# A state-space mixer on one Trainium2 core: the way from the input projection into the chunk loop, in another order

## The chip, the core and the metric

The kernel runs on one core of one Trainium2 chip. Such a core has five engines with an instruction queue each: TensorE (PE, matrix products; its weight loads are listed apart as PEld), VectorE (DVE), ScalarE (ACT), GpSimd (POOL) and SyncE (SP, which here only starts transfers). The queues run by themselves and meet at semaphores. The metric is the device time of one execution in microseconds (us), lower is better.

## The reference

The program is four blocks on one sequence of 1024 tokens with 256 features: a Mamba-like mixer with a feed-forward block, a factor mixing, a grouped-query attention and a mixture of experts. The change is in the mixer. Cut to what matters:

```python
h = _rmsnorm(hidden_states, ln1_w)
zxbcdt = h @ W_in                       # (1024 x 256) @ (256 x 770)
z, xv, Bv, Cv, dt = jnp.split(zxbcdt, splits, axis=-1)
xBC = jnp.concatenate([xv, Bv, Cv], axis=-1)          # 512 features
conv = sum((xp[:, k:k + l, :] * conv_w[k] for k in range(D_CONV))) + conv_b
xBC = jax.nn.silu(conv)
dt = jax.nn.softplus(dt + dt_bias)      # 2 columns, one for each head
a = -jnp.exp(A_log)
dA = dt * a
y = _ssd(xh * dt[..., None], dA, Bh, Ch, CHUNK)       # 8 chunks of 128 tokens
y = y + D[None, None, :, None] * xh
y = _rmsnorm(y * jax.nn.silu(z), norm_w)
h = res + y @ W_out
```

`_ssd` goes over the chunks; each needs cumulated sums of `dA`, exponentials of them, three products inside the chunk and a state that is handed to the next one.

## The kernel before

Each engine has its own hand-written program; the order of the work on an engine is the order of the code, and what it waits for is written as `wait_ge` on a semaphore.

**Projection.** The 1024 tokens are two groups (g = 0, 1) of 512. The 6 x 128 wide columns of `W_in` give twelve fills of a PSUM bank, in the order of `IN_FILLS`: q = 0 to 3 are the four blocks that are convolved (`CONV_BLOCKS`) for group 0, q = 4 to 7 the same for group 1, q = 8 to 11 the two blocks of z for both groups. Fill q goes to bank `2 + q % 4`, so that fill q waits for the evacuation of fill q - 4 (`s_evac`). On PE a fill is two matmuls of 128x512 (line 1409), and the trace has two records for each f32 matmul, so four records. Between fills 1 and 2 PE transposes the second group of normalised rows (line 1388). The two `dt` columns are 16 narrow matmuls of 128x2 (line 1403, 32 records), two for each of the eight tiles of 128 tokens, into bank 6; before, all of them stand ahead of fill 4, and the last one releases `s_dtp`.

**Evacuation, on ACT** (`projected`, lines 645 and 646): a fill that is convolved is copied to `xpad` and written once more as the last tap plus bias to `cv`; a fill of z goes through one Silu (line 642).

**Convolution, on DVE** (`convolve(g, pair)`, line 984): two blocks of one group, three taps each, so six instructions of 128x512. It waits for the evacuation of its two fills. ACT finishes it with a Silu for each block (`convolved(g, pair)`, line 656, `s_xbc`).

**Step sizes.** `dt` is a softplus, made as Exp on ACT (line 665), one added on DVE (line 998), Ln on ACT (line 670) and some ten small DVE instructions with 128x16 elements (lines 991 to 1012). The last gives `dA`. POOL makes the ramps of chunks 0 and 1 from it (line 490), PE two narrow products (lines 1416 and 1417), of which ACT takes the Exp (line 679), and DVE `dt` times the decay (line 1016), which POOL uses for `ddx` (line 505).

**Chunk loop.** For chunk c, `front(c)` on PE makes two transposes (line 1429), the segment sums (lines 1435 to 1437) and the product of B and C (line 1440). ACT copies the transposes to `tok` (line 693) and takes the Exp of the sums (line 695). DVE multiplies both with `dt` (`masked(c)`, line 1026). `back(c)` on PE makes the state and y (lines 1448 to 1456), and DVE and ACT finish them (lines 1045 to 1057, 685). `front(c + 1)` stands ahead of `back(c)`. The splits of the feed-forward weights (`ffn_w_hi` on ACT, `ffn_w_lo` on DVE) are done between chunks.

Table loads of ACT (ACT_TABLE_LOAD in the trace) are put in by the compiler where the next function isn't in the loaded set.

Of the kernel before, what the change touches and what calls it, by code (L numbers as in the profile page):

```python
# [29 lines left out]
ACT = mybir.ActivationFunctionType  # L30
# [4 lines left out]
TT = T // P  # L35
# [6 lines left out]
H_SSD = 2  # L42
N_IN = 770
CONV_BLOCKS = 4
# [29 lines left out]
def build(nc, x_in, small_in, const_in, w_in, w_out, f_w13, f_w2, factors, ffn_bias, wq, wk, wv, wo,  # L74
          gate, m_w1, m_w3, m_w2, m_w2t, out):
    slots_in = nc.dram_tensor("expert_in", [SLOT_TILES * P, SLOT_W], F32, kind="Internal").ap()
    with ExitStack() as ctx:
# [534 lines left out]
        def _(act):  # L612
# [51 lines left out]
            act.wait_ge(s_dtv, 1)  # L664
            nc.scalar.activation(dts[3], dts[3], ACT.Exp).then_inc(s_dta, 1)
            nc.scalar.activation(ea_log[:, :], small[:, C_ALOG:C_ALOG + H_SSD], ACT.Exp).then_inc(s_dta, 1)
            for q in range(4, 6):
                projected(q)
            act.wait_ge(s_dtv, 2)
            nc.scalar.activation(dts[5], dts[4], ACT.Ln).then_inc(s_dta, 1)  # L670
            for q in range(6, 8):
                projected(q)
            for g, pair in ((0, 0), (0, 1), (1, 0)):
                convolved(g, pair)
            for q in range(2 * CONV_BLOCKS, len(IN_FILLS)):
                projected(q)
            convolved(1, 1)
            act.wait_ge(s_decp, 1)
            nc.scalar.activation(dec_t[:, :], ps[:, 6, 0:2 * TT * H_SSD], ACT.Exp).then_inc(s_dec, 1)

            def squares(c):
                act.wait_ge(s_yg, c + 1)
# [5 lines left out]
            def chunk(c):  # L688
                b = c % 2
                act.wait_ge(s_front_tr, c + 1)  # L690
                if c >= 2:
                    act.wait_ge(s_st, c - 1)
                nc.scalar.copy(tok[:, b], ps[:, 0, 0:2 * P]).then_inc(s_tok, 1)
                act.wait_ge(s_front_seg, c + 1)
                nc.scalar.activation(decays[:, b], ps[:, 2, :], ACT.Exp).then_inc(s_exp, 1)

# [179 lines left out]
        def _(dve):  # L876
# [98 lines left out]
            def convolve(g, pair):  # L975
# [3 lines left out]
                for k in range(TAPS - 1):  # L979
                    for c in (2 * pair, 2 * pair + 1):  # L980
                        if k:
# [5 lines left out]

            convolve(0, 0)
            convolve(0, 1)
            dve.wait_ge(s_dtp, 1)  # L990
            link(V.tensor_tensor(dts[6], ps[:, 6, 64:64 + TT * H_SSD].rearrange("p (t h) -> p t h", h=H_SSD),
                                 row(C_DTB), ALU.add))
            V.scalar_tensor_tensor(dts_t[:, 48:64], dts_t[:, 96:112], -1.0, dts_t[:, 96:112], ALU.mult,
                                   ALU.min).then_inc(s_dtv, 1)
            convolve(1, 0)

            dve.wait_ge(s_dta, 1)
            V.tensor_scalar(dts[4], dts[3], 1.0, None, ALU.add).then_inc(s_dtv, 1)
            dve.wait_ge(s_dtv, 2)
# [11 lines left out]
            link(V.tensor_scalar(ea_log[:, :], ea_log[:, :], -1.0, None, ALU.mult))  # L1011
            V.tensor_tensor(dts[1], dts[0], ea_log[:, :].unsqueeze(1).broadcast_to([P, TT, H_SSD]),
                            ALU.mult).then_inc(s_dtv, 1)
            convolve(1, 1)
            dve.wait_ge(s_dec, 1)
            V.tensor_tensor(dts[2], dec[:, 0], dts[0], ALU.mult).then_inc(s_dd, 1)
# [358 lines left out]
        def _(pe):  # L1375
            mm = nc.tensor.matmul

            def transposes(ph, g):
# [10 lines left out]
                                                   hh[:, t, k * P:(k + 1) * P], ident)  # L1389
                last.then_inc(s_tr, 1)  # L1390

            pe.wait_ge(s_ident, 16)
            transposes(PH_MIX, 0)
            pe.wait_ge(s_win, 16)
            for q, (g, fb) in enumerate(IN_FILLS):
                if q < 2 * CONV_BLOCKS and q % CONV_BLOCKS == 0:
                    pe.wait_ge(s_hT, g + 1)
                if q == 2:
                    transposes(PH_MIX, 1)
                if q == CONV_BLOCKS:  # L1400
                    for t in range(TT):
                        for k in range(KD):
                            last = mm(ps[:, 6, 64 + H_SSD * t:64 + H_SSD * (t + 1)], hT[:, k, t * P:(t + 1) * P],
                                      win_sb[:, k, 6 * P:], start=(k == 0), stop=(k == KD - 1))
                    last.then_inc(s_dtp, 1)
                if q >= 4:
                    pe.wait_ge(s_evac, q - 3)
                for k in range(KD):
                    last = mm(ps[:, 2 + q % 4, :], win_sb[:, k, fb * P:(fb + 1) * P],  # L1409
                              hT[:, k, g * GW:(g + 1) * GW], start=(k == 0), stop=(k == KD - 1))  # L1410
                last.then_inc(s_proj, 1)
# [7 lines left out]
            def front(c):  # L1419
                cols = slice(c * P, (c + 1) * P)  # L1420
                if c == 0:
                    pe.wait_ge(s_cbf, 1)
                    pe.wait_ge(s_evac, len(IN_FILLS))
                if c in (0, GT):
                    pe.wait_ge(s_xbc, (c // GT + 1) * CONV_BLOCKS)
                if c >= 1:
                    pe.wait_ge(s_tok, c)
                for k in range(2):
                    last = nc.tensor.transpose(ps[:, 0, k * P:(k + 1) * P], cv[:, k, cols], ident)
                last.then_inc(s_front_tr, 1)  # L1430
                pe.wait_ge(s_ramp, c + 1)
                if c >= 1:
                    pe.wait_ge(s_exp, c)
                rmp = ramp[:, c % 2]
                mm(ps[:, 2, 0:2 * P], gt_m, rmp, start=True, stop=False)
                mm(ps[:, 2, 0:2 * P], ident_b[:, :], neg_s[:, :], start=False, stop=True)
                mm(ps[:, 2, 2 * P:4 * P], ones, rmp, start=True, stop=True).then_inc(s_front_seg, 1)
                if c >= 1:
                    pe.wait_ge(s_mt, c)
                mm(ps[:, 1, 0:2 * P], cv[:, 1, cols], cv[:, 2:4, cols], start=True, stop=True).then_inc(s_front_g, 1)  # L1440

            def back(c):
                b = c % 2
                if c >= 1:
                    pe.wait_ge(s_state, c)
                if c < TT - 1:
# [383 lines left out]
```

## Time and profile before

| | us |
|---|---|
| median of 3 runs | 572.33 |
| lowest and highest run | 569.45, 575.76 |
| the profiled execution | 575.39 |
| its span on the core | 573.6 |
| outside of the span | 1.8 |

Over the span PE is busy for 510.1 us (89%), DVE for 354.0 us (62%), ACT for 277.5 us (48%) and POOL for 171.5 us (30%). The part that is changed lies in the first 52 us. Times below are microseconds from the start of the span of this one execution. The granted clock of TensorE is given as a share of its full speed: 1.00 is 2.4 GHz, 0.50 is 1.2 GHz.

### The profile page before, as it was taken

Reading aid. Unit: us, or ns where it says so; the run is one execution under the profiler, and the core shown is the slowest. Engines: PE = TensorE matmul, PEld = TensorE weight load, DVE = VectorE, ACT = ScalarE, POOL = GpSimd, SP = SyncE. Lnnn points to the kernel's source line nnn. Section 1 sums busy time; section 2 is a strip of 40 time slices with the busy share of each in tenths; the row PEclk is TensorE's granted clock in tenths of the full one; section 3 lists DMA queues with packets and bytes.
Section 4 is the critical chain, followed back from the end, with each engine's and each line's share of the span. In section 5 each row is a group of like instructions: output and inputs, shape, how many; then the busy total and the mean of one; then the engine's idle time right before and its main releaser. Section 6 shows DMA issues by size and latency. Waiting matters only on the chain.

```text
span 573.6 us, 9705 instructions
## 1 busy us (share of the span) xinstructions
PE 510.1 (89%) x3168; PEld 415.3 (72%) x3169; DVE 354.0 (62%) x864; ACT 277.5 (48%) x526; POOL 171.5 (30%) x229
## 2 busy tenths in 40 slices
PE   3988988999998999898999999635999999999994
PEld 2537766787796876676777878524788888888883
DVE  5873656746654633664676777455777777777761
ACT  1565432323502345555566465105666666666661
POOL 3013413995002202333131111120133333333332
PEclk9997979999999996999999999866999999999998
DMA  9997002000001009500000000981122222222212
GB/s 340 390 338 241 2 0 75 0 1 0 1 1 37 1 0 395 230 29 29 20 20 20 20 11 29 350 291 48 28 39 36 35 31 37 32 37 36 35 19 26
DMA packets 25812, 47.46 MB, mean 83 GB/s; under 512 B 2224, under 2 KB 21168, under 8 KB 25392
## 3 DMA queue, kind: packets, MB, share of 16 engines
q1 hardware_dynamic: 21408, 41.76, 20.7%
q0 software_dynamic: 4080, 5.15, 6.4%
q8 instruction: 21, 0.34, 0.3%
q10 hardware_dynamic: 288, 0.08, 0.1%
q14 instruction: 15, 0.12, 0.1%
HBM read 32.01 MB, written 14.98 MB: 82 GB/s over the span
## 4 chain that ended last, share of the span: by engine, by line
PE 67%; DVE 12%; POOL 7%; ACT 6%; issue 6%; DMA 1%; POOLq 0%; SPq 0%; ACTq 0%; DVEq 0%
PE ps L1701 16%; PE ps L1721 10%; PE ps L1602 5%; PE ps L1617 4%; PE ps L1587 4%; PE ps L1560 4%; PE ps L1507 3%; PE ps L1634 3%; PE ps L1409 3%; PE ps L1709 3%; PE ps L1526 2%; PE ps L1564 2%; POOL early L528 2%; POOL early L536 2%; POOL rows L523 1%
## 5 line engine op out<-in xcount | busy, mean ns | idle before, releaser
L1701 PE MATMUL ps<-split,xsT 128*128 128x512 f32 (+1 forms) x414 | 95.6, 385 | 1.0 <-DVE split L1322 1.0
L1701 PEld LDWEIGHTS ps<-split,xsT 128*128 128x128 f32 x414 | 76.5, 192 | 13.4 <-issue 1.2
L1322 DVE TENSOR_TENSOR split<-early,split 128x1408 fp32r<-128x1408 f32 x46 | 72.8, 1622 | 5.9 <-ACT split L823 5.3
L1721 PE MATMUL ps<-mid,work 128*128 x276 | 63.4, 379 | 0.8 <-ACT work L812 0.8
L823 ACT CAST split<-early 128x1408 fp32r x46 | 62.6, 1364 | 0.7 <-issue 0.7
L1172 DVE TENSOR_REDUCE nmax<-ps 128x1 f32<-128x128 f32 (+7 forms) x64 | 45.4, 751 | 24.6 <-PE ps L1587 24.4
L595 POOL TENSOR_TENSOR rstd<-mhalf 128x1 f32<-128x1 f32 x23 | 21.4, 929 | 119.8 <-ACT work L819 119.8
L1721 PEld LDWEIGHTS ps<-mid,work 128*128 128x128 f32 x276 | 52.0, 190 | 7.0 <-issue 1.0
L1304 DVE TENSOR_TENSOR work<-work,ps 128x704 f32<-128x704 f32 x23 | 20.4, 888 | 44.6 <-PE ps L1701 44.6
L808 ACT ACTIVATE work<-ps 128x704 f32<-128x704 f32 x22 | 16.8, 762 | 48.2 <-PE ps L1701 48.2
L757 ACT ACTIVATE work<-ps,nmax 128x128 f32<-128x128 f32 (+7 forms) x48 | 35.9, 751 | 2.9 <-DVE nmax L1172 2.9
L596 POOL DMA_INDIRECT out<-work,slot_i x23 | 35.8, 1557 | 4.1 <-issue 2.3
L1602 PE MATMUL ps<-cst,work 128*128 128x128 f32 x216 | 32.7, 285 | 2.2 <-DVE work L1178 1.0
L765 ACT COPY work<-ps 128x512 f32<-128x512 f32 (+3 forms) x32 | 16.2, 506 | 34.2 <-PE ps L1602 33.6
L1602 PEld LDWEIGHTS ps<-cst,work 128*128 128x128 f32 x216 | 24.7, 144 | 8.0 <-ACT work L757 4.5
L572 POOL DMA_INDIRECT expert_in<-rows,slot_i x16 | 16.3, 1018 | 47.5 <-DVE slot_i L1252 45.0
L730 ACT ACTIVATE work<-ps 128x512 f32<-128x512 f32 x16 | 9.6, 598 | 38.5 <-PE ps L1507 38.5
L1409 PE MATMUL ps<-rows,early 128*128 128x512 f32 x48 | 25.6, 691 | 1.6 <-ACT rows L628 1.5
L476 POOL TENSOR_TENSOR rstd<-veps,mhalf 128x4 f32<-128x4 f32 x8 | 8.1, 1034 | 59.1 <-DVE veps L907 45.7
L1507 PE MATMUL ps<-hT_hi,ffn_w_hi 128*128 128x512 f32 x64 | 20.1, 396 | 3.4 <-DVE early L1101 1.8
L765 ACT COPY rows<-ps 128x512 f32<-128x512 f32 (+3 forms) x32 | 16.3, 508 | 14.1 <-PE ps L1602 13.6
L553 POOL CAST q_hi<-mid 128x128 fp32r<-128x128 f32 x32 | 9.9, 310 | 43.6 <-PE ps L1587 43.1
(254 smaller groups left out, 1104.9 us busy)
## 6 DMA issues: line engine op xcount, KB each, us to landing
early<-m_w SPq DMA_DIRECT2D x16, 704.0 KB, 9.4
expert_in<-pad SPq DMA_DIRECT2D x8, 1040.0 KB, 12.7
mid<-m_w SPq DMA_DIRECT2D x8, 640.0 KB, 9.4
work<-expert_in SPq DMA_DIRECT2D x23, 130.0 KB, 2.9
early<-factors SPq DMA_DIRECT2D x1, 2048.0 KB, 11.2
early<-wq SPq DMA_DIRECT2D x1, 2048.0 KB, 15.6
mid<-f_w SPq DMA_DIRECT2D x1, 2048.0 KB, 19.9
rows<-x_in SPq DMA_DIRECT2D x4, 256.0 KB, 3.7
```

Of the source, the lines that this page charges most:

```text
L596: nc.gpsimd.indirect_dma_start(out=out, out_offset=bass.IndirectOffsetOnAxis(ap=dest_now[:, b:b + 1], axis=0), in_=ey[:, b], in_offset=Non ...
L757: nc.scalar.activation(probs[u % 4][:, 0:w], score_row(u), ACT.Exp, bias=nmax[:, u:u + 1], accum_out=psums[:, u:u + 1]).then_inc(s_pr, 1)
L765: nc.scalar.copy(pT[u % 4][:, 0:w], ps[:, pT_banks(u), 0:w]).then_inc(s_pT, 1)
L823: nc.scalar.copy(split_w[0][:, :, w * I:(w + 1) * I], expert_w(e, w)).then_inc(s_whi[w], 1)
L1172: V.tensor_reduce(nmax[:, u:u + 1], score_row(u), AX_X, ALU.max, negate=True).then_inc(s_max, 1)
L1322: V.tensor_tensor(lo, expert_w(e, w), hi.bitcast(F32), ALU.subtract).then_inc(s_wlo[w], 1)
L1409: last = mm(ps[:, 2 + q % 4, :], win_sb[:, k, fb * P:(fb + 1) * P], hT[:, k, g * GW:(g + 1) * GW], start=(k == 0), stop=(k == KD - 1))
L1507: last = mm(ps[:, 2 + 2 * w + q % 2, :], fw13_split[pw][:, w * KD + k, f * P:(f + 1) * P], hT_split[ph][:, k, g * GW:(g + 1) * GW], start= ...
L1560: last = mm(bank, qkv_w[pw][:, j // 4, at:at + P], hT_split[ph][:, k, g * GW:(g + 1) * GW], **ends)
L1602: last = nc.tensor.transpose(ps[:, pT_banks(u) + j // 4, (j % 4) * P:(j % 4 + 1) * P], probs[u % 4][:, j * P:(j + 1) * P], ident)
L1701: last = mm(up_flat[:, c0:c1], xsT[px][b][:, k, :], split_w[pw][:, k, c0:c1], start=(k == 0 and px == pw), stop=(k == KD - 1 and px == 1))
L1721: last = mm(ps[:, 6, 0:D], eaT[:, b, c, :], we[:, c, :], start=(c == 0), stop=(c == IB - 1))
```

## The change

It leaves every operation as it is and moves some:

- on DVE, the rest of the step sizes (lines 998 to 1012) goes ahead of `convolve(1, 0)`;
- on ACT, the Silus of the convolution stand between the evacuations of later fills, and the Exp of the decays stands behind the first copy to `tok`;
- on PE, the 16 narrow products are spread: two tiles' worth (four matmuls) each ahead of fills 1, 3, 4 and 5; each lot releases `s_dtp` once, and DVE waits for all four;
- `front(0)` on PE waits for nine evacuations in place of twelve (fill 8 is the last in bank 2, which it overwrites), and `back(0)` for all twelve.

```diff
@@ ACT
-            for q in range(4, 6):
-                projected(q)
+            projected(4)
             act.wait_ge(s_dtv, 2)
             nc.scalar.activation(dts[5], dts[4], ACT.Ln).then_inc(s_dta, 1)
-            for q in range(6, 8):
-                projected(q)
-            for g, pair in ((0, 0), (0, 1), (1, 0)):
-                convolved(g, pair)
-            for q in range(2 * CONV_BLOCKS, len(IN_FILLS)):
+            projected(5)
+            convolved(0, 0)
+            projected(6)
+            convolved(0, 1)
+            projected(7)
+            projected(8)
+            convolved(1, 0)
+            for q in range(9, len(IN_FILLS)):
                 projected(q)
             convolved(1, 1)
-            act.wait_ge(s_decp, 1)
-            nc.scalar.activation(dec_t[:, :], ps[:, 6, 0:2 * TT * H_SSD], ACT.Exp).then_inc(s_dec, 1)
...
                 nc.scalar.copy(tok[:, b], ps[:, 0, 0:2 * P]).then_inc(s_tok, 1)
+                if c == 0:
+                    act.wait_ge(s_decp, 1)
+                    nc.scalar.activation(dec_t[:, :], ps[:, 6, 0:2 * TT * H_SSD], ACT.Exp).then_inc(s_dec, 1)
@@ DVE
-            dve.wait_ge(s_dtp, 1)
+            dve.wait_ge(s_dtp, 4)
...
-            convolve(1, 0)
-
             dve.wait_ge(s_dta, 1)
...
+            convolve(1, 0)
             convolve(1, 1)
@@ PE
+            DT_TILES = {1: (0, 1), 3: (2, 3), 4: (4, 5), 5: (6, 7)}
...
-                if q == CONV_BLOCKS:
-                    for t in range(TT):
+                if q in DT_TILES:
+                    for t in DT_TILES[q]:
...
-                    pe.wait_ge(s_evac, len(IN_FILLS))
+                    pe.wait_ge(s_evac, 2 * CONV_BLOCKS + 1)
...
             def back(c):
                 b = c % 2
+                if c == 0:
+                    pe.wait_ge(s_evac, len(IN_FILLS))
```

ACT from the Exp of the step sizes to the Exp of the first segment sums, before. `early<-ps` is an evacuation (two rows for a fill that is convolved), `early<-early` a Silu of the convolution, `dts` the step sizes:

```order
L665 ACTIVATE dts<-dts 128x16 [waits dt_vector]
...
L670 ACT_TABLE_LOAD
L670 ACTIVATE dts<-dts 128x16 [waits dt_vector]
...
L646 ACTIVATE early<-ps,small 128x512
L656 ACT_TABLE_LOAD
L656 ACTIVATE early<-early 128x512 [waits conv_tap] x6
L642 ACTIVATE early<-ps 128x512 [waits in_proj] x4
L656 ACTIVATE early<-early 128x512 [waits conv_tap] x2
L679 ACT_TABLE_LOAD
L679 ACTIVATE dec<-ps 128x32 [waits decay_sum]
L693 COPY mid<-ps 128x256 [waits chunk_transposed]
L695 ACTIVATE mid<-ps 128x512 [waits segments]
```

The six Silus in one row are now pairs with evacuations between them, one fill less stands ahead of the Ln, and the Exp of the decays follows the copy. After:

```order
L669 ACT_TABLE_LOAD
L669 ACTIVATE dts<-dts 128x16 [waits dt_vector]
L645 COPY early<-ps 128x512 [waits in_proj]
L646 ACTIVATE early<-ps,small 128x512
L656 ACT_TABLE_LOAD
L656 ACTIVATE early<-early 128x512 [waits conv_tap] x2
...
L642 ACTIVATE early<-ps 128x512 [waits in_proj]
L656 ACTIVATE early<-early 128x512 [waits conv_tap] x2
L642 ACTIVATE early<-ps 128x512 [waits in_proj] x3
L656 ACTIVATE early<-early 128x512 [waits conv_tap] x2
L693 COPY mid<-ps 128x256 [waits chunk_transposed]
L696 ACT_TABLE_LOAD
```

What moved: fill 5 went behind the Ln, fills 6, 7 and 8 between pairs of Silus, and the first copy of the chunk loop ahead of the last table load.

PE between the first two fills and fill 4, before (`rows,early` is a fill, `cst,rows` a transpose, `early,rows` a narrow product; each fill is two rows):

```order
L1409 MATMUL ps<-rows,early 128x512 x3
L1388 MATMUL ps<-cst,rows 128x128 [waits normalised,feature_major]
...
L1409 MATMUL ps<-rows,early 128x512 x4
L1403 MATMUL ps<-early,rows 128x2 [waits feature_major]
L1403 MATMUL ps<-early,rows 128x2 x15
L1409 MATMUL ps<-rows,early 128x512 [waits in_evac]
```

After:

```order
L1412 MATMUL ps<-rows,early 128x512
L1406 MATMUL ps<-early,rows 128x2 x4
L1412 MATMUL ps<-rows,early 128x512 x2
...
L1412 MATMUL ps<-rows,early 128x512 x2
L1406 MATMUL ps<-early,rows 128x2 x4
L1412 MATMUL ps<-rows,early 128x512 x2
L1406 MATMUL ps<-early,rows 128x2 [waits feature_major]
L1406 MATMUL ps<-early,rows 128x2 x3
```

What moved: eight of the sixteen narrow matmuls now stand ahead of fill 3, four of them right behind the very first fill.

## Rows read from the trace of the kernel before

**Rows 1.** The chain that ended last, 0 to 120 us: start, length, engine and line.

```profile
17.41 0.87 PE ps L1388 x8
18.28 3.44 PE ps L1409 x8
21.71 3.47 PE ps L1403 x32
25.18 5.25 PE ps L1409 x8
...
31.75 4.06 DVE early L984 x6
...
39.77 3.23 ACT early L656 x6
43.01 1.95 ACT early L642 x4
45.04 0.66 PE ps L1429 x2
...
50.67 0.61 ACT mid L695
```

**Rows 2.** The timeline, weight loads and matmuls of the first fills: start, length.

```profile
11.33 6.07 PE L1409 MATMUL ps<-rows,early 128*128 128x512 f32 x8 [1.51 <-ACT rows L628]
...
14.88 0.34 PEld L1409 LDWEIGHTS ps<-rows,early 128*128 128x128 f32 x1 [0.52 <-issue]
...
15.73 0.34 PEld L1409 LDWEIGHTS ps<-rows,early 128*128 128x128 f32 x1 [0.52 <-issue]
...
16.38 0.19 PEld L1409 LDWEIGHTS ps<-rows,early 128*128 128x128 f32 x1 [0.31 <-issue]
```

**Rows 3.** The timeline, DVE: `convolve(0, 1)`, `convolve(1, 1)` and `masked` of chunks 0 and 1.

```profile
23.05 4.06 DVE L984 SCALAR_TENSOR_TENSOR early<-early,small 128x512 f32<-128x512 f32 x6 [0.24 <-ACT early L646]
...
38.50 4.48 DVE L984 SCALAR_TENSOR_TENSOR early<-early,small 128x512 f32<-128x512 f32 x6 [0.43 <-ACT early L646]
...
48.52 0.61 DVE L1026 SCALAR_TENSOR_TENSOR mid<-ps,dts,mid 128x128 f32<-128x128 f32 x2 [0.82 <-PE ps L1440]
...
51.37 0.61 DVE L1026 SCALAR_TENSOR_TENSOR mid<-ps,dts,mid 128x128 f32<-128x128 f32 x2 [2.24 <-ACT mid L695]
```

**Rows 4.** The timeline, ACT, from the first Exp of the step sizes on.

```profile
27.44 0.22 ACT L665 ACTIVATE dts<-dts 128x16 f32<-128x16 f32 x1 [4.42 <-DVE dts L993]
...
27.65 0.57 ACT L645 COPY early<-ps 128x512 f32<-128x512 f32 x1
...
28.12 0.78 ACT L646 ACTIVATE early<-ps,small 128x512 f32<-128x512 f32 x1
...
35.94 0.22 ACT L670 ACTIVATE dts<-dts 128x16 f32<-128x16 f32 x1 [2.92 <-DVE dts L998]
...
36.06 0.57 ACT L645 COPY early<-ps 128x512 f32<-128x512 f32 x1
...
37.66 0.80 ACT L646 ACTIVATE early<-ps,small 128x512 f32<-128x512 f32 x1
...
38.48 1.28 ACT L656 ACT_TABLE_LOAD   x1
...
46.00 1.28 ACT L679 ACT_TABLE_LOAD   x1
...
47.66 0.60 ACT L695 ACTIVATE mid<-ps 128x512 f32<-128x512 f32 x1
```

**Rows 5.** Stretches: length, busy time of PE, PEld, DVE, ACT, POOL, clock, DMA share, GB/s.

```profile
26.00:27.00 1.00, 1.00 (x3) 0.50 (x2) 1.00 (x2) 0.00 (x0) 0.00 (x0) 0.70 1.02 274
...
46.00:47.00 1.00, 1.00 (x5) 0.64 (x4) 0.00 (x0) 1.00 (x1) 0.00 (x0) 0.50 1.10 335
...
91.20:94.60 3.40, 1.77 (x8) 1.16 (x8) 2.35 (x6) 2.55 (x3) 0.00 (x0) 1.00 0.58 171
```

**Rows 6.** The timeline, POOL: the ramps of chunks 0 and 1.

```profile
38.15 1.63 POOL L490 TENSOR_TENSOR mid<-cst,dts 128x256 f32<-128x256 f32 x2 [24.32 <-DVE dts L1012]
```

## The prediction

> **What bounds the kernel now.** I read the chain of waits first, for which engine ends last on the way to the first chunk; then the timeline of ACT, DVE and PE there, for the length of each step; then the stretches, for the granted clock. Over the whole span PE carries most of the chain, but the change touches only its first 52 us, and there the chain hops. [rows 1] show it: fills on PE, the narrow products (3.47 us), fills 4 and 5 (5.25 us), then the evacuation of fill 5, `convolve(1, 0)` on DVE (4.06 us), later six Silus in a row on ACT (3.23 us for six, so 0.54 us each), four Silus of z (1.95 us), and only then, at 45.04, `front(0)` on PE. Two waits stand out. ACT holds a table loaded but may take the Ln of the step sizes only at 35.94, since DVE does all of `convolve(1, 0)` before the one added that the Ln needs: 2.92 us of idle time [rows 4]. And fills 6 and 7 are evacuated behind that Ln, so `convolve(1, 1)` starts only at 38.50 [rows 3]. What the loop waits for at its start is `masked(0)` at 48.52, released by PE's product of B and C, and `masked(1)` at 51.37, released by the Exp of the segment sums (ACT at 50.67) [rows 1, 3]. PE makes both with half the clock (0.50 in the stretch from 46 us) [rows 5], as it had nothing to do from 41 us on. From `masked(1)` on DVE, ACT and PE go round in a fixed pattern, and what follows the loop starts when it ends, so I take it that what is won up to `masked(1)` is won at the end. The sum is made against the profiled execution, 575.39 us, of which 573.6 us are the span; the median of the runs is 572.33 us, 3.06 us lower, and the gain is taken off that.
>
> **The change, part by part.** The same operations run, and the number of table loads is the same; what counts is when each starts.
>
> *Narrow products (a loss).* A fill at full clock takes 1.72 us (four of eight records in 3.44 us), a narrow lot of eight records 0.87 us (3.47 us for 32) [rows 1]. Before, all 32 stand behind fill 3. Now a lot stands ahead of fill 1 and one ahead of fill 3. The first fill runs at the low level: weight loads 0.85 us apart at 14.88 and 15.73, the next after 0.65 us at 16.38, so the clock rose near 16.1, after 4.8 us of wide products from 11.33 on [rows 2] (the clock column doesn't show this first low stretch; the records do). Fill 0 ends at 11.33 + 4 x 0.85 = 14.7. A lot at the low level costs at most twice 0.87, so 1.7 us; with the rise at 16.1 as before it ends at 16.3, and fill 1 at 18.0 instead of 17.4 by the chain, which I count as 0.7 us later. The second lot adds 0.87 us. So fill 3 is evacuated 1.6 us later, `convolve(0, 1)` starts at 24.65 instead of 23.05 [rows 3], and the first Exp of the step sizes at 27.44 + 1.6 = 29.05 [rows 4]. The lots ahead of fills 4 and 5 are hidden: ACT takes these fills only behind that Exp.
>
> *Step sizes ahead of `convolve(1, 0)`, Silus between evacuations (a gain).* From 29.05 on ACT is a row without a wait: both small Exps 0.21 us (27.44 to 27.65), fill 4 1.25 us (27.65 to 28.90), table load 1.28, Ln 0.12 (35.94 to 36.06), fill 5 1.25, table load 1.28, two Silus 1.08, fill 6 1.25, two Silus 1.08, fill 7 1.25 [rows 1, 4]. Sum 10.05, so fill 7 is evacuated at 39.1, where it was 38.46 before. That step alone is 0.6 us late. The cover for it: DVE does the small instructions and `convolve(1, 0)` meanwhile, from fill 5 at 33.3 on, 4.06 us or 4.48 us beside POOL's ramps of 1.63 us [rows 3, 6], until 37.8 at most. Then `convolve(1, 1)` runs from 39.1, now without the ramps beside it, 4.06 us, to 43.15. Before, ACT still had six Silus, four of z and two more to do one behind another when it was done; now all but the last two Silus are through, and ACT waits for DVE. The last Silu, which starts with the end of the last tap and takes 0.6 us, ends at about 43.8, where the last table load could start at 46.00 before: 2.2 us earlier.
>
> *The Exp of the decays behind the copy.* Between the last Silu and the end of the first Exp of the segment sums lay 46.00 to 48.26, 2.26 us [rows 4]; the same four instructions run in another order, so I take 2.3 us, to 46.1. The first copy is about 1.2 us earlier against the rest, which hides `ddx(0)` on POOL. Behind the new wait for the decay sums on ACT the Exp of the segments is queued, but PE has made both by then.
>
> *`front(0)` waits for nine evacuations.* PE's last fill waits for fill 7 and ends at 39.1 + 1.7 = 40.8, the narrow sums and `front(0)` follow by 43 or so at full clock, 3 us before ACT is through. Even with the old wait for twelve (z is through at about 42) it would end near 44.2. So this edit is worth nothing by itself; it would cost or save at most the 1.2 us between, and only if PE were slow. The same goes for the wait in `back(0)`.
>
> *Start of the loop.* `masked(0)` moves from 48.52 to 46.1, 2.4 us, as it waits for ACT and no more for PE. The segment sums of chunk 1 on PE wait for the Exp of chunk 0. Before, they began about 48.9 and the Exp behind them at 50.67 [rows 1], 1.8 us at the low clock. PE now idles from 43 to 46, as it did before its `front(0)`, and at half clock there [rows 5]; I take the low level again: 46.1 + 1.9 = 48.0, Exp of 0.6 us, `masked(1)` at 48.75 instead of 51.37 [rows 3]. That is **2.6 us** less. At full clock it would be 0.9 us more, 3.5 us; with nothing of it but the 0.6 us by which fill 7 is late, and `masked` bound as before, the change is worth less than zero. These are the ends for the order alone. I take 2.6: it is nearest to the rows, each step having its own.
>
> *Table loads.* In the rows a load ends 1.28 us after it starts, and starts 0.02 us behind the end of the instruction ahead of it (37.66 + 0.80 = 38.46, load at 38.48) [rows 4]. So I count 1.28 us for each of the three that now stand on ACT's path, of which one stood in the shadow of a wait before. The Trainium skill (ScalarE: Activation LUTs, What ACT_TABLE_LOAD costs) gives 1283 ns for the load and 1380 ns more for a drain with it, 2.66 us for each switch. By that page the load that is newly on the path would cost 1.38 us more and the gain would be an estimated 1.2 us; the trace agrees with the load and shows no drain.
>
> **The rivals.**
>
> *The clock rises later.* For: ahead of the rise the engine had only wide products, and now a narrow lot stands behind the first fill; and behind the 3.47 us of narrow products the clock fell (0.70 in the stretch from 26 us, and fills 4 and 5 took 5.25 us against 3.44 us for two at full clock) [rows 1, 5]. So narrow products do not keep it up, and may not raise it. Against: the first fill alone is 3.4 us of wide products. Then fill 1 runs at the low level too and ends 1.7 us later (3.44 for 1.72); all behind it moves by that, and the gain is 0.9 us: 571.4.
>
> *The clock falls under fills 10 and 11.* These wait for fills 6 and 7, and PE idles 1.8 us and 0.5 us there. If it falls, they take 3.4 us each, z is evacuated at about 44.3, and the last Silus, which stand behind z on ACT, and `front(0)` at the low level, end the way in: `masked(0)` at about 48, gain 0.6 us: 571.7. Against: PE was busy for 1.77 of 3.4 us from 91.2 on and kept 1.00 [rows 5].
>
> *Full clock into the loop*: gain 3.5 us, 568.8. For: the idle time ahead of the sums is 3 us in two pieces, where before it was 3.6 us in one.
>
> *Slower: the clock stays low until fill 3.* The place is the stretch from the first narrow lot on. With it low, fills 1, 2, 3 cost 1.7 us more each, the transposes (0.87 us at full clock) 0.87 and the second lot 0.87: 6.9 us. From that the 2.6 us go off: 4.3 us slower, 576.6. Each microsecond for which the low level lasts longer costs 0.5 us, so this decides from about 5.2 us behind 16.1 on, when the clock is still low at 21.3. Against: fill 1, fill 2 and the transposes stand together in between, as they do before.
>
> *It does nothing that can be seen.* The gain is real but the executions differ by more: 569.45 to 575.76 for one kernel. That is no case with a time of its own, but it widens the range.
>
> **How the numbers follow.** As forecast 0.50; later rise 0.22; low under the last fills 0.10; full clock into the loop 0.10; slower 0.05; something else 0.03. The forecast is 572.33 - 2.6 = 569.7 us. The cases that hold most run from 568.8 to 571.7; the median of a few runs of either kernel can itself be off by some 2 us, as three runs lay within 3.4 us of their median. So the range is 566.5 to 573.7. About 1% (5.7 us) is what a measurement of this kernel can tell from no change. Faster by that much needs twice the forecast, by luck of the runs: 0.07. Slower by that needs the slower case and more: 0.03. Within 1%: 0.90.
>
> **What the profile will show.** Right: the first Exp of the step sizes near 29.0; the Ln near 31.9 without a wait; fill 7 evacuated near 39; `convolve(1, 1)` 4.1 us long; the last Silu ended near 43.8; `masked(0)` near 46.1, released by ACT; `masked(1)` near 48.8; the loop and all behind it as long as before. Wrong: fill 1 ended at 19.5 or later (late rise); a record of fill 11 longer than 0.5 us (clock fell); or `masked(1)` early but the end of the loop not, if something behind has a time of its own, such as a transfer. It would also be wrong if ACT, now without a pause from 29 to 41 us, found its Silus waiting for a tap.

## The result, and the profile after

The changed kernel takes 577.09 us (median of 15 runs, 570.48 to 580.09), the kernel before, timed beside it, 572.75 us (15 runs, 569.07 to 581.21). The ratio is 1.0065 with a 95% interval of 1.0039 to 1.0091, so **0.65% slower, 3.7 us**, where 2.6 us less was forecast. The ratios, and the means below, leave out the runs that took over 1.5% more than the fastest run of the same kernel. A second measurement (e5 below) gave 1.0062 (1.0027 to 1.0096). The profiled execution took 575.79 us, its span 574.0 us.

The timeline of PE in the trace after, the first fills. They answer to [rows 2]:

```profile
11.26 3.75 PE L1412 MATMUL ps<-rows,early 128*128 128x512 f32 x4 [1.51 <-ACT rows L628]
14.80 1.70 PE L1406 MATMUL ps<-early,rows 128*128 128x2 f32 x8
16.37 3.71 PE L1412 MATMUL ps<-rows,early 128*128 128x512 f32 x4
19.92 1.04 PE L1390 MATMUL ps<-cst,rows 128*128 128x128 f32 x8
```

All of fill 1 (from 16.37) runs at the low level, and so does the narrow lot ahead of it (1.70 us; the later lots take 0.95 us by the same view). Fill 1 ends at 19.9 us, where it ended at 17.4 before. The timelines of ACT and DVE after, for [rows 4] and [rows 3] (the one on DVE starts with `convolve(1, 0)`):

```profile
31.01 0.22 ACT L665 ACTIVATE dts<-dts 128x16 f32<-128x16 f32 x1 [4.43 <-DVE dts L996]
...
33.79 0.21 ACT L669 ACTIVATE dts<-dts 128x16 f32<-128x16 f32 x1
...
35.17 1.28 ACT L656 ACT_TABLE_LOAD   x1
...
44.44 1.29 ACT L656 ACTIVATE early<-early 128x512 f32<-128x512 f32 x2 [0.49 <-DVE early L987]
...
46.00 1.28 ACT L696 ACT_TABLE_LOAD   x1
```

```profile
35.24 4.77 DVE L987 SCALAR_TENSOR_TENSOR early<-early,small 128x512 f32<-128x512 f32 x6
...
41.00 4.07 DVE L987 SCALAR_TENSOR_TENSOR early<-early,small 128x512 f32<-128x512 f32 x6 [0.99 <-ACT early L646]
...
48.09 0.61 DVE L1028 SCALAR_TENSOR_TENSOR mid<-ps,dts,mid 128x128 f32<-128x128 f32 x2 [0.39 <-ACT mid L698]
...
50.08 0.61 DVE L1028 SCALAR_TENSOR_TENSOR mid<-ps,dts,mid 128x128 f32<-128x128 f32 x2 [1.38 <-ACT mid L698]
```

The chain is the forecast one, 2 us late: the first Exp at 31.01 (forecast 29.05), the Ln without a wait 2.78 us behind it, `convolve(1, 1)` from 41.00, the last table load at 46.00, no earlier than before. `masked(0)` waits for ACT and no more for PE, and `masked(1)` is at 50.08, still 1.3 us earlier than before. The timeline of SP gives where the mixer's gain is: the loads of the expert weights start with the attention, and the first rows are stored 21 us later (columns: start, length). After:

```profile
211.90 3.94 SPq L402 DMA_DIRECT2D early<-m_w  x8
...
232.90 125.66 SPq L409 DMA_DIRECT2D out<-rows  x7
```

and before:

```profile
214.23 4.26 SPq L402 DMA_DIRECT2D early<-m_w  x8
...
232.76 124.66 SPq L409 DMA_DIRECT2D out<-rows  x7
```

So the attention starts 2.3 us earlier and its first rows are stored 0.1 us later. The stretches of PE show what lies between (length, PE busy and instructions, granted clock, DMA share, GB/s). After:

```profile
218.00:219.00 1.00, 1.00 (x8) 0.50 0.99 411
229.00:230.00 1.00, 1.00 (x8) 0.50 1.02 417
213.00:233.00 20.00, 19.30 (x108) 0.57 1.00 406
```

and before:

```profile
229.00:230.00 1.00, 1.00 (x14) 1.00 1.02 417
213.00:233.00 20.00, 18.64 (x128) 0.74 0.90 358
```

The clock was low for 17.0 us (214.5 to 231.5) after, and for 10.2 us (217.6 to 227.8) before.

### The profile page after: what moved, and what is told of

The parts are those of the page before. It is cut to its first block, busy times and chain, and to the rows that moved or that the text cites. A ratio compares the mean times of both kernels' runs of the same rounds, so it can differ in the third digit from the quotient of the medians.

```text
span 574.0 us, 9706 instructions
## 1 busy us (share of the span) xinstructions
PE 510.3 (89%) x3168; PEld 415.6 (72%) x3169; DVE 354.4 (62%) x864; ACT 277.3 (48%) x526; POOL 171.9 (30%) x229
## 4 chain that ended last, share of the span: by engine, by line
PE 65%; DVE 12%; POOL 7%; ACT 7%; issue 6%; DMA 1%; POOLq 0%; SPq 0%; ACTq 0%; DVEq 0%
PE ps L1706 16%; PE ps L1726 10%; PE ps L1607 5%; PE ps L1622 5%; PE ps L1592 4%; PE ps L1565 4%; PE ps L1512 3%; PE ps L1714 3%; PE ps L1639 2%; PE ps L1531 2%; PE ps L1569 2%; PE ps L1412 2%; POOL early L528 2%; POOL early L536 2%; DVE early L987 1%
## 5 line engine op out<-in xcount | busy, mean ns | idle before, releaser
L1174 DVE TENSOR_REDUCE nmax<-ps 128x1 f32<-128x128 f32 (+7 forms) x64 | 45.5, 752 | 26.4 <-PE ps L1592 26.2
L811 ACT ACTIVATE work<-ps 128x704 f32<-128x704 f32 x22 | 16.7, 759 | 48.3 <-PE ps L1706 48.3
L760 ACT ACTIVATE work<-ps,nmax 128x128 f32<-128x128 f32 (+7 forms) x48 | 35.9, 750 | 2.9 <-DVE nmax L1174 2.9
L1512 PE MATMUL ps<-hT_hi,ffn_w_hi 128*128 128x512 f32 x64 | 20.2, 397 | 3.2 <-DVE early L1103 1.7
```

The costliest lines, as they stand in the source:

```text
L760: nc.scalar.activation(probs[u % 4][:, 0:w], score_row(u), ACT.Exp, bias=nmax[:, u:u + 1], accum_out=psums[:, u:u + 1]).then_inc(s_pr, 1)
L1174: V.tensor_reduce(nmax[:, u:u + 1], score_row(u), AX_X, ALU.max, negate=True).then_inc(s_max, 1)
L1512: last = mm(ps[:, 2 + 2 * w + q % 2, :], fw13_split[pw][:, w * KD + k, f * P:(f + 1) * P], hT_split[ph][:, k, g * GW:(g + 1) * GW], start= ...
```

## The experiments

The kernel before was timed beside each batch: 571.36 us (29 runs) for e1 to e4, 571.68 (23) for e5 to e8, 571.82 (29) for e9 to e12, 570.15 (23) for e13 to e16. Ratios are to it, with their 95% intervals. The batches were timed on different chips, and the times come in clusters, so that a median of few runs can jump by 2 us. Where kernels of two batches are compared, the means are therefore given too. That of the changed kernel is 575.2 us (25 runs, the first 15 and e5), that of the kernel before 571.3 us (115 runs).

**e1, the kernel before again.** No edit.

> The kernel before, unchanged, for a second trace and more times. Theory L (the time behind 212 us depends on when the granted clock falls there, and that differs from execution to execution): the times spread over 569 to 581 us again, in clusters, and the second trace shows the low stretches at other places or of other lengths than the first (which had 217.5 to 227.7 us, and 10.2 us long). Theory D (everything behind the loop has a fixed length, the spread is something else): the low stretches lie where they lay, to 1 us.

571.64 us, 0.9999 (0.9959 to 1.0038). The clock didn't fall in the attention's first steps at all, and the stretch up to the first stored row took 14.4 us instead of 18.6:

```profile
215.78 4.16 SPq L402 DMA_DIRECT2D early<-m_w  x8
...
230.16 0.34 SPq L409 DMA_DIRECT2D out<-rows  x1
```

So one and the same program loses between nothing and 4 us there. Theory D is out for the kernel before.

**e2, the changed kernel with a pure delay behind the mixer.**

```diff
             pool.wait_ge(s_wq, 16)
+            for junk in (ddx[:, 0], ddx[:, 1], ramp[:, 0])[:3]:
+                nc.gpsimd.tensor_tensor(junk, wq_sb[:, 1, 0:256], wq_sb[:, 2, 0:256], ALU.add)
             for r in range(1, QH):
```

> The changed kernel with three additions of 128x256 more on POOL ahead of the sums of the query weights, about 0.85 us each and all on POOL's chain from 96 to 132 us, so 2.5 us of pure delay behind the mixer. The attention then starts about where it starts in the kernel before. Theory L (the 2.3 us won by 212 us in the trace were lost since the attention then met the clock at a worse moment): the median is that of the kernel before, 572.7 us or up to 2 us over it, so faster than the changed kernel (577.1) in spite of more work. Theory D (the change costs a fixed 3.7 us somewhere): 577.1 + 2.5 = 579.6 us.

576.94 us (6 runs), 1.0120 (1.0074 to 1.0166): neither number, by the medians. But the 577.1 us without the delay is a median too, and it lies in the upper cluster of its times. By the means the delay added 2.2 us (577.35 against 575.17, give or take 1.4), by the ratios 0.56% (3.2 us). So this run doesn't speak against D, which wants 2.5 us more, and it speaks against L: the time didn't return to that of the kernel before. The trace has a second use: here the clock rose early, and the front came out 0.3 to 0.9 us better than forecast.

```profile
14.47 0.95 PE L1408 MATMUL ps<-early,rows 128*128 128x2 f32 x8
15.28 1.96 PE L1414 MATMUL ps<-rows,early 128*128 128x512 f32 x4
...
28.17 0.22 ACT L667 ACTIVATE dts<-dts 128x16 f32<-128x16 f32 x1 [4.42 <-DVE dts L998]
...
45.23 0.61 DVE L1030 SCALAR_TENSOR_TENSOR mid<-ps,dts,mid 128x128 f32<-128x128 f32 x2 [0.38 <-ACT mid L700]
...
48.42 0.61 DVE L1030 SCALAR_TENSOR_TENSOR mid<-ps,dts,mid 128x128 f32<-128x128 f32 x2 [2.58 <-PE ps L1445]
```

The lot takes 0.8 us and fill 1 1.8 us. The first Exp was forecast at 29.05, `masked(0)` at 46.1 and `masked(1)` at 48.75, the last one behind segment sums at the low level, as here (low from 44.8 to 48.2).

**e3, the changed kernel with the narrow products together.**

```diff
-            DT_TILES = {1: (0, 1), 3: (2, 3), 4: (4, 5), 5: (6, 7)}
+            DT_TILES = {4: range(TT)}
-            dve.wait_ge(s_dtp, 4)
+            dve.wait_ge(s_dtp, 1)
```

> The changed kernel with the narrow products in one row ahead of fill 4 again (one wait for them on DVE); the other orders stay as changed. In the trace of the changed kernel fill 1 ended at 19.9 us with all records at the low level, so I expect here: fill 1 at 17.3, first Exp of the step sizes at 27.4 (31.0 there), masked(0) near 44.6 (48.1 there, 48.5 before), masked(1) near 46.7. By theory L the total can go either way, by up to 5 us against the 3.5 us that are won; by theory D it is 577.1 - 3.5 = 573.6 us.

572.67 us, 1.0027 (0.9995 to 1.0059). Fill 1 ends at 17.0, the first Exp is at 27.22, `masked(0)` at 44.5 and `masked(1)` at 46.5, as expected to 0.3 us. The total is 4.4 us under 577.1 by the medians, 2.6 us by the means (give or take 1.7) and 0.38% (2.2 us) by the ratios. The rest of the order is worth what was forecast of it and more (4.9 us at `masked(1)` against [rows 3]); the lots of narrow products take 3.6 us of that back (50.1). And still the total isn't under the kernel before: its attention starts at 209.9, 4.3 us earlier, and its clock was low there for 17.0 us.

**e4, the kernel before with only the narrow products spread.** The `DT_TILES` of the changed kernel and its wait for all four lots, put into the kernel before.

> The kernel before with only the narrow products spread. The two lots ahead of fill 3 and the later rise of the clock should put the first Exp of the step sizes at 31.0 us instead of 27.4, and as fills 4 to 7 are not late on PE, masked(0) moves by less, to about 50 us from 48.5. By theory D the total is 1.5 to 3.5 us over the kernel before, 575 us; by theory L it can be anything from 570 to 580.

572.86 us, 1.0027 (0.9987 to 1.0066), first Exp at 31.33, `masked(0)` at 50.6: the front as expected, late by 3.9 us at the first Exp, 2.1 at `masked(0)` and 1.5 at `masked(1)`. The median shows 1.5 us of it, inside the interval; in the trace the clock didn't fall in the attention's first steps.

**e5, the changed kernel again.** No edit.

> The changed kernel, unchanged, for a second trace and more times. Theory L (the mixer is shorter, and what is lost is lost to the granted clock in the attention's first steps and in front of the experts): masked(1) near 48.4 us if the clock rose in fill 1 near 16 us, near 50.1 if it rose near 19.6, and the attention's start at 211 to 213 us either way, under the 214.2 and 215.8 us of the kernel before. Theory D (a fixed cost behind the mixer): the stretches from the attention's start on have the lengths of the first trace, 21.0 us up to the first stored row.

575.56 us, 1.0062 (1.0027 to 1.0096). Again fill 1 is late (evacuated from 19.9), `masked(1)` at 49.9, the attention starts at 213.4 and takes 19.5 us to the first stored row, with 13.6 us of low clock. Theory D wanted 21.0 us for that stretch, so it is out for the changed kernel too.

**e6 and e7, the clock held up in the attention's first steps**, in the kernel before and in the changed one.

```diff
                 banks = [score_banks(2 * m + h) for h in range(2)]
+                if m < 12:
+                    for _ in range(4):
+                        mm(ps[:, banks[0], 3 * P:4 * P], ones, gt_m, start=True, stop=True, skip_group_check=True)
                 pe.wait_ge(s_qs, m + 1)
```

> The kernel before with four extra f32 matmuls of 128x128 in each of the first 12 steps of the attention, put where PE is about to wait for the split queries; their results are overwritten by the scores. They cost up to 0.9 us of PE a step, 10 us in all if none were hidden; at full clock about half should be. Theory L: the low stretch in the first steps (10.2 us in one trace of this kernel, none in another) doesn't come, and the times spread less. Theory D: the spread stays.

> The changed kernel with the same extra matmuls. Theory L: no low stretch in the first steps, and against the other kernel with the extra matmuls it is faster, by the 2 to 3 us by which its attention starts earlier. Theory D: it is slower than that one by the 3.7 us by which the changed kernel was slower than the kernel before.

576.44 us (6 runs) and 578.97 us (6 runs). The clock held in both; the stretches of the changed kernel with them:

```profile
213.00:233.00 20.00, 19.18 (x168) 1.00 0.81 321
```

The stretch up to the first stored row takes 21.0 us in both, as long as with 17 us of low clock, so the extra matmuls are an instrument and no mend. But the kernel with the change was 2.5 us slower than the one before by the medians (1.1 us by the ratios, and the times overlap), where theory L as I had it wanted it faster: not all of the loss lies behind the attention's start. In e7 the front was in its worst case: fill 1 late, and then `front(1)` at the low level too (47.6 to 54.4):

```profile
48.34 1.19 PE L1438 MATMUL ps<-mid,cst 128*128 128x256 f32 x2 [1.65 <-ACT mid L698]
```

so that `masked(1)` came at 51.5.

**e8, the delay of e2 in the kernel before.**

> The kernel before with three more additions on POOL's chain between 96 and 132 us, 2.5 us of pure delay. Without the clock it is 2.5 us over the kernel before. Theory L: anything between no change and 7 us more, since the attention then starts at another moment; the same addition left the changed kernel at 576.9 us (577.1 without), so a delay need not show.

578.57 us, 1.0108 (1.0068 to 1.0147). 2.5 us of delay cost 6.2 us here by the ratio (3.9 to 8.4; 6.9 us by the medians), against 2.2 us in e2. The total doesn't follow one to one what is added or saved ahead of the attention.

**e9 and e10, the clock raised before the first fill**, with the matmuls of e6 and e7.

```diff
             pe.wait_ge(s_ident, 16)
+            pe.wait_ge(s_x[0], 16)
+            for _ in range(2):
+                mm(ps[:, 7, :], ident, x[:, 0:2, :].rearrange("p t d -> p (t d)"), start=True, stop=True)
             transposes(PH_MIX, 0)
+            for _ in range(1):
+                mm(ps[:, 7, :], ident, x[:, 0:2, :].rearrange("p t d -> p (t d)"), start=True, stop=True)
```

> The kernel before with the extra matmuls in the attention's first steps (as in the kernel before with them, 576.4 us) and three more ahead: two wide ones (128x512, of the identity and the raw rows) before the first transposes, one behind them, all into a bank that is free. Theory R (the moment at which the granted clock rises in the first fills sets the front): fill 1 is evacuated near 15 us instead of 17.4, and the total falls by about 2 us, to 574.5. If the clock doesn't rise earlier for it, nothing changes but up to 0.3 us more.

> The changed kernel with the same matmuls, in the attention and ahead (579.0 us with those in the attention alone). Theory R (four of five traces with a narrow lot behind the first fill had the low level until 19.6 us and fill 1 evacuated at 20, against 17.4 with the lots together): with the clock up before fill 0 the lot costs 0.9 us and no more; fill 1 near 16, first Exp of the step sizes near 27, and the kernel is 1.5 to 2.6 us faster than the kernel before with the same matmuls. Theory M (the low level in the first fills is not what costs; something else of the order is slower): it stays 2.5 us slower than that one.

577.85 us (6 runs) and 574.92 us (12 runs), on one chip. In both the clock was up before fill 0 and fill 1 was evacuated from 15.0 and 15.8 us. The kernel before gained nothing, against my expectation (576.44 without). Its 32 narrow products in a row follow, and the clock fell at 23.3 us and again for 10.3 us at the loop's end; as it did so in other traces of this kernel too, why nothing was gained isn't shown. The changed kernel gained 4.0 us against e7 by the medians, 3.4 us (give or take 0.9) against the mean of e7 and e14, and is **2.9 us faster than the kernel before** with the same matmuls: with the clock up ahead, the order gives about what was forecast for it (3.3 us by the means, give or take 1.6). Theory M is out.

**e11, the edit of e3 with the matmuls of e7.**

> The changed kernel with the narrow products in one row ahead of fill 4 again and the extra matmuls in the attention. Against the changed kernel with the extra matmuls (579.0 us) theory R wants 3.5 us less, since the trace with the products together had masked(1) at 46.5 us against 50.0: 575.5 us, and 1 us under the kernel before with them (576.4). Theory M: 578 to 579.

575.80 us, as theory R said: 3.2 us under e7 by the medians, and 2.6 us (give or take 1.2) under the mean of e7 and e14.

**e12, a mend**: narrow products in two lots ahead of fills 4 and 5, and the three wide matmuls of e10 ahead, nothing in the attention.

```diff
-            DT_TILES = {1: (0, 1), 3: (2, 3), 4: (4, 5), 5: (6, 7)}
+            DT_TILES = {4: (0, 1, 2, 3), 5: (4, 5, 6, 7)}
```

> A mend: the changed kernel with the narrow products in two lots, four tiles ahead of fill 4 and four ahead of fill 5, so that none stands between fills that ACT is waiting for, and with the three wide matmuls ahead of the first fill, without those in the attention. Front: fill 1 evacuated near 15 us, first Exp near 25, masked(1) near 45, so 6 us earlier than in the kernel before. The total is open to the clock in the attention's first steps: 565 to 573 us; 568 if the gain went through on average.

568.61 us, 0.9969 (0.9934 to 1.0005) of the kernel before. `masked(1)` is at 46.0, 5.4 us earlier than in [rows 3], and the attention starts at 209.3. Of that 3.2 us show by the medians and 1.8 us by the ratio, whose interval reaches 1. So it isn't shown that this kernel beats the one before.

**e13 and e14, e6 and e7 again.** No new edit.

> The kernel before with the extra matmuls in the attention once more, on one chip with the next two, since its first six times (576.0 to 580.9 us) and the changed kernel's (577.7 to 580.5) overlap. Theory R: 576.5 us.

> The changed kernel with them once more. Theory R, front alone: 579 us, 2.5 over the kernel before with them, so that some two thirds of the 3.7 us are in the front and the rest comes from the clock behind the attention's start. Theory L alone (the front is faster, all of the loss lies behind): 575 us, 1 to 2 under it.

576.80 us, as expected, and 577.36 us, between what the two theories said (6 runs each). Pooled with e6 and e7, twelve times each, the means are 577.6 and 578.1 us and the medians 576.6 and 577.7. So with the clock held in the attention the changed kernel is slower by 0.6 us by the means and 1.1 us by the medians; with 12 times each the difference is uncertain by 1.3 us, and none isn't excluded. The trace of e14 has the early rise again (fill 1 from 15.48, `masked(1)` at 48.6).

**e15, the two lots of e12 with the matmuls of e7 alone.**

> The changed kernel with the narrow products in two lots ahead of fills 4 and 5 and with the extra matmuls in the attention. Theory R: none of the lots delays a fill that ACT waits for, and the clock rises in fill 1; 3.5 to 4.5 us under the changed kernel with them, 575 us.

574.87 us (12 runs): the expected time, though only 2.5 us under e14, where 3.5 to 4.5 were expected, and 1.9 us under e13. Only the places of the narrow lots differ from e14.

**e16, the changed kernel with only the three wide matmuls ahead.**

> The changed kernel as it is, with only the three wide matmuls ahead of the first fill. Theory R: the late rise is what the order lost by, so with the clock up the front is 4 us shorter (first Exp of the step sizes at 26.7 us, as with those in the attention, against 31.0); the total falls from 577 to 573 on average, give or take 2 us for the clock behind. Theory M: it stays at 577.

569.56 us, 0.9989 (0.9950 to 1.0029) of the kernel before, more than I expected. Three matmuls on an idle PE take 0.76% (4.3 us) off the changed kernel, by the two ratios. The timeline of PE:

```profile
4.04 3.75 PE L1398 MATMUL ps<-rows,cst 128*128 128x512 f32 x4 [4.04 <-DMA rows<-x_in]
...
11.21 1.96 PE L1417 MATMUL ps<-rows,early 128*128 128x512 f32 x4 [0.41 <-ACT rows L628]
13.00 0.95 PE L1411 MATMUL ps<-early,rows 128*128 128x2 f32 x8
13.81 1.96 PE L1417 MATMUL ps<-rows,early 128*128 128x512 f32 x4
```

Fill 0 takes 1.8 us instead of 3.5, the lot 0.8 instead of 1.6, fill 1 1.8 instead of 3.5.

All traces in one table. The columns are the start of the evacuation of fill 1, the starts of `masked(1)`, of the attention (first load of expert weights) and of the first stored row, the end of the span, and how long the clock was low between the second and the third; us.

| kernel, trace | fill 1 | masked(1) | attention | first row | end | low |
|---|---|---|---|---|---|---|
| before | 17.4 | 51.4 | 214.2 | 232.8 | 573.6 | 10.2 |
| before, e1 | 18.1 | 51.9 | 215.8 | 230.2 | 568.5 | 0 |
| before + 2.5 us, e8 | 16.7 | 50.8 | 219.2 | 236.2 | 576.6 | 6.8 |
| spread alone, e4 | 20.1 | 52.9 | 216.5 | 230.9 | 574.6 | 0 |
| after | 20.1 | 50.1 | 211.9 | 232.9 | 574.0 | 17.0 |
| after, e5 | 19.9 | 49.9 | 213.4 | 232.9 | 571.3 | 13.6 |
| after + 2.5 us, e2 | 17.3 | 48.4 | 215.3 | 233.6 | 574.8 | 10.3 |
| together, e3 | 17.2 | 46.5 | 209.9 | 230.8 | 573.9 | 17.0 |
| two lots, e12 | 14.4 | 46.0 | 209.3 | 230.2 | 572.7 | 17.0 |
| after, wide ahead, e16 | 15.8 | 46.6 | 209.0 | 230.0 | 571.0 | 17.1 |
| held: before, e6 and e13 | 17.4, 16.8 | 48.8, 50.9 | 212.3, 215.8 | 233.3, 236.8 | 574.3, 579.1 | 0 |
| held: after, e7 and e14 | 20.2, 17.5 | 51.5, 48.6 | 216.0, 212.1 | 237.0, 233.1 | 577.6, 575.5 | 0 |
| held: e9, e10 | 15.0, 15.8 | 49.1, 47.0 | 213.9, 210.4 | 234.9, 231.4 | 577.5, 573.9 | 0 |
| held: e11, e15 | 16.5, 16.4 | 47.0, 45.5 | 211.7, 208.7 | 232.7, 229.6 | 575.2, 572.1 | 0 |

Over the traces without the held clock the attention starts anywhere in 7.5 us (209.0 to 216.5, without e8), but the first row is stored within 3.6 us (230.0 to 233.6): whoever comes early has the long low stretch. With the clock held, what is behind the attention's start takes 361.6 to 363.6 us in all eight, whatever the front did; without, 352.7 to 364.0.

The record has more than the traces: the span and the mean granted clock of every run, not only of the profiled one. From them comes the time at the low level, 2 x (1 - clock) x span. It leaves out the low stretch ahead of the first rise, which the clock column doesn't have, and so it leaves out a late rise. Within a kernel, one us more at the low level goes with 0.33 us more of span (give or take 0.02, fitted over 191 runs without the held clock; for the first 15 runs of the kernel before no clocks are on record). Means, us:

| kernel | runs | low | span, against before | of it by the low time | at equal low time |
|---|---|---|---|---|---|
| before, with e1 | 103 | 47.4 | | | |
| after, with e5 | 25 | 53.8 | +4.0 | +2.1 | +1.9 (0.4) |
| spread alone, e4 | 11 | 47.8 | +2.1 | +0.1 | +2.0 (0.6) |
| together, e3 | 12 | 55.6 | +1.5 | +2.7 | -1.2 (0.6) |
| after, wide ahead, e16 | 12 | 50.4 | -0.7 | +1.0 | -1.7 (0.5) |
| two lots, e12 | 12 | 50.5 | -1.0 | +1.0 | -2.0 (0.5) |
| before + 2.5 us, e8 | 10 | 56.9 | +6.4 | +3.1 | +3.3 (0.6) |
| after + 2.5 us, e2 | 6 | 52.8 | +6.2 | +1.7 | +4.5 (0.8) |

The last column has its 95% uncertainty in brackets. It is an association and no experiment, and the low time counts wherever it lies, so that a low stretch in the front counts with the rest. But it sorts the runs. The delay is worth 3.3 and 2.5 us (4.5 less 1.9) at equal low time, near the 2.5 us that were put in. The spread alone costs as much as the whole change. And without the spread, or with the clock up ahead, the order is 1.2 to 2.0 us faster.

## Why the prediction was wrong, point by point

**Narrow products: the step that failed first, by its size and by its case.** I took the rise at 16.1 us "as before" and called the late rise a rival of 0.22, priced at 1.7 us. It was the more frequent case: of six traces with a narrow lot behind fill 0 and without the wide matmuls ahead (after, e2, e4, e5, e7, e14), four have it, and none of the eight with the first lot behind fill 3 (before, e1, e3, e6, e8, e11, e13, e15). It costs 2.6 us against the early case (fill 1 evacuated from 19.9 to 20.2, against 17.3 and 17.5), since the lot itself also runs to its end at the low level. In the early case the clock was up already in the lot (0.8 us), so that fill 1 wasn't late at all, where the sum had 0.7 us for it. That the place of the lots is what costs is shown by e3, e11 and e15, and by e4 at equal low time; that it costs by way of the clock, by e10 and e16, where the lot stays and the loss goes.

**Step sizes and Silus: right.** The row on ACT was forecast at 10.05 us from the first Exp to the evacuation of fill 7; after, it is 31.01 to 40.97, 9.96 us. `convolve(1, 1)` took 4.07 us (forecast 4.06), `masked(0)` follows ACT, 7.1 us behind its start (forecast 7.0). `convolve(1, 0)` beside the ramps took 4.77 us, not 4.48; it was hidden. Fills 10 and 11 ran at the full level (1.8 us each), so the rival of a fall under them didn't come.

**Table loads: right.** Each took 1.28 us and the next instruction followed at once (load at 35.17, 0.02 us behind the end of the evacuation), on ACT's path too. The drain of 1380 ns that the Trainium skill adds (ScalarE: Activation LUTs, What ACT_TABLE_LOAD costs) isn't in any of these traces: where an instruction was ready, it started 0.01 or 0.02 us behind the load in all 18. The trace decides.

***front(0)*: not tested by itself.** In the trace after it ended 3 us ahead of ACT, as forecast; no run takes the wait for nine alone.

**Start of the loop: right in mechanism.** With the early rise `masked(1)` came at 48.4 and 48.6 (forecast 48.75). That `front(1)` may run at either level was foreseen, with 0.9 us between them; it is 1.2 us (`masked(1)` follows `masked(0)` by 3.2 us in e2 and by 2.0 in the trace after, where the level was full). With the late rise and the low level together it came at 51.5, where [rows 3] have 51.4.

**One trace as the base: a miss.** I took the front of the kernel before from one execution. `masked(1)` there is at 51.4, 51.9, 50.8, 50.9 and 48.8 in five traces: where the clock doesn't fall behind the narrow products, its Ln is at 34.3 instead of 35.9. Against this mean of 50.8 the changed kernel's five (50.1, 49.9, 48.4, 51.5, 48.6, mean 49.7) win 1.1 us and not 2.6. By the twelve times with a held clock even that isn't seen (0.6 to 1.1 us lost, uncertain by 1.3), and at equal low time the change costs 1.9 us. As e4 costs the same, that part goes with the spread; and as e16 has the same spread with the clock up ahead and is 1.7 us faster at equal low time, it goes with the late rise, which this low time doesn't count. Why five traces show the front even and the runs don't isn't settled; five traces of each kernel are few for a rise that comes at either of two moments, and the kernel before has low stretches in its front that count as low time.

**"What is won up to masked(1) is won at the end": the step that failed most.** I gave no reason for it but the fixed pattern of the loop. It holds as far as the attention (2.3 us in the first pair of traces) and no further. Without a held clock, what is behind the attention's start takes 362.1, 357.9 and 359.5 us in the three traces of the changed order and 359.4, 352.7 and 357.4 in those of the kernel before: 3.3 us more on average, though the two groups overlap. With the clock held that difference is gone. Over its runs the changed kernel has 6.3 us more at the low level, which goes with 2.1 of the 4.0 us, and in the traces it has less of it in the front than the kernel before, not more. So half of the loss or more is the granted clock behind the attention's start, of which I had no case; my "slower" rival had another place. What stays open: why the changed kernel meets the long low stretch more often than chance would have it. An early start goes with a long one in the table, and the times come in clusters that are clusters of the clock: before, 568.4 to 570.3 us in four of ten runs, all with a mean clock of 0.960 to 0.965; changed, 577.1 to 577.9 us in 11 of 27 runs, all with 0.945 or 0.946. A rule for it wasn't shown.

## What to carry to other kernels

Where the granted clock moves as it does here, a saving ahead of a sparse stretch isn't a saving at the end: look at the granted clock in every sparse stretch behind the change, and at more than one trace of the kernel before, before the sum is carried to the end. Be wary of narrow products behind the very first wide ones, while the clock still has to rise; try some wide ones on an idle TensorE ahead of them (it gave 4.3 us here, and nothing in the kernel whose narrow products stand in one row). Compare the mean granted clock of all runs along with their times: a median of clustered times made a delay of 2.5 us look like nothing in e2. And if two kernels are to be compared for one stage, holding the clock in the later stages of both takes most of the other differences away.

## What the runs showed of the hardware

- The level of the granted clock at one place differs between executions of one program: low for 10.2 us or not at all in the attention's first steps of the kernel before, and 17.0 or 13.6 us in the changed one.
- Over the 191 runs of the kernels without the held clock, one us more at the low level went with 0.33 us more of span.
- With three wide f32 matmuls (128x512) more, two of them from 4.0 us on, fill 0 ran at the full level from its start (1.8 us long in e16). Without them it took 3.2 to 3.5 us, and the level came up between 14 and 17 us or between 19 and 21. They lay in time in which PE otherwise did only transposes or nothing.
- The same 2.5 us of delay cost 6.2 us in one kernel (e8) and 2.2 us in the other (e2).
- Six convolution taps of 128x512 (SCALAR_TENSOR_TENSOR) on DVE took 4.77 us beside POOL's ramps where they took 4.06 or 4.07 alone.
